# Second attention: the root's function table is loaded directly behind the gate's function

## What is computed

```python
def _L1_attn_ref(x, Wq, Wk, Wv, Wg, Wo, gn_w, gn_b):
    ...
    retention = jnp.einsum('bhsd,bhtd->bhst', q, k) * SCALING
    ...
    out = jnp.einsum('bhst,bhtd->bhsd', retention, v)
    out = out.transpose(0, 2, 1, 3).reshape(B * S, H, Dh)
    mean = out.mean(axis=-1, keepdims=True)
    var = out.var(axis=-1, keepdims=True)
    out = (out - mean) * jax.lax.rsqrt(var + EPS)
    out = out * gn_w.reshape(H, Dh) + gn_b.reshape(H, Dh)
    out = out.reshape(B, S, D)
    gate = jax.nn.silu(x @ Wg.T)
    return gate * out @ Wo.T
```

## Time and profile before

| | |
|---|---|
| three executions | 1035.74, 1040.65, 1041.17 us; median 1040.65 us |
| profiled execution, first to last instruction (span) | 1034.5 us |
| busy in the span: TensorE (matmul), VectorE, ScalarE, GpSimd | 855.4, 859.7, 629.3, 736.5 us |
| the second attention in the span | from 376.5 us (its first table load) to 677.7 us (the next stage's first) |
| one batch of it, once it runs evenly | 17.27 us (from one gate's load at 438.98 us to the next at 456.25 us) |
| function table loads in the whole program | 40, of 1283 ns each, 32 of them in the loop of batches of the second attention |

### The profile page before, as it was taken

The page is one execution under the profiler, slowest core; times in us unless marked ns, Lnnn a source line. Parts: engine busy times, 40 slices in busy tenths (PEclk is TensorE's granted clock), DMA queues, the critical chain, the costliest instruction groups (busy, mean ns, idle before and its releaser), DMA issues. The chain is left out here.

```text
span 1034.5 us, 25463 instructions
## 1 busy us (share of the span) xinstructions
PE 855.4 (83%) x5240; PEld 612.9 (59%) x5240; DVE 859.7 (83%) x2837; ACT 629.3 (61%) x1652; POOL 736.5 (71%) x642
## 2 busy tenths in 40 slices
PE   5699999999969968989898989558888733999993
PEld 4466666666636745555555555335655533999993
DVE  5589999999977976989888889778899861899995
ACT  2655555555429946676767675467765203998992
POOL 4488888888854528999999999655598471355554
PEclk9899999999989979999999999969999755999997
DMA  9520000000000000000000000264567564544420
GB/s 247 172 63 1 0 0 0 0 0 0 1 4 1 1 0 1 11 21 10 20 10 20 10 20 10 59 162 108 167 208 214 185 223 125 151 132 133 134 64 21
DMA packets 64935, 70.11 MB, mean 68 GB/s; under 512 B 8965, under 2 KB 52178, under 8 KB 64740
## 3 DMA queue, kind: packets, MB, share of 16 engines
q1 hardware_dynamic: 50612, 47.20, 16.5%
q0 software_dynamic: 6368, 16.89, 4.8%
q10 hardware_dynamic: 7872, 5.08, 2.0%
HBM read 32.32 MB, written 24.50 MB: 55 GB/s over the span
## 5 line engine op out<-in xcount | busy, mean ns | idle before, releaser
L473 PE MATMUL a_pS<-a_kv,utri 128*128 128x360 f32 (+3 forms) x768 | 263.1, 479 | 17.6 <-POOL a_kv L464 7.2
L464 POOL TENSOR_TENSOR a_kv<-a_qk,a_vv 128x1152 f32<-128x1152 f32 (+1 forms) x128 | 263.9, 2063 | 13.3 <-DVE a_qk L438 13.3
L473 PEld LDWEIGHTS a_pS<-a_kv,utri 128*128 128x128 f32 x768 | 135.5, 190 | 98.8 <-issue 24.6
L569 POOL TENSOR_TENSOR a_tt<-a_tt 128x576 f32<-128x576 f32 (+1 forms) x128 | 156.7, 1225 | 48.2 <-DVE a_tt L553 44.3
L553 DVE TENSOR_TENSOR a_tt<-a_pS,a_qk 128x360 f32<-128x360 f32 (+3 forms) x384 | 180.8, 526 | 9.1 <-PE a_pS L473 6.3
L1950 POOL DMA_INDIRECT out_dram<-x_o,x_place x71 | 69.4, 977 | 75.9 <-DVE x_o L1937 71.4
L581 DVE TENSOR_REDUCE a_nd<-a_tt 128x144 f32<-128x720 f32 (+3 forms) x128 | 104.3, 815 | 0.0
L519 ACT ACTIVATE a_tt<-a_pI 128x144 f32<-128x144 f32 (+1 forms) x96 | 40.1, 417 | 105.3 <-PE a_pI L481 105.2
L512 PEld LDWEIGHTS a_pO<-wgate,a_yT 128*128 128x128 f32 x256 | 44.6, 192 | 75.7 <-issue 42.5
L1530 POOL DMA_INDIRECT ys<-m_S,m_dest x64 | 62.9, 984 | 33.5 <-issue 12.5
L512 PE MATMUL a_pO<-wgate,a_yT 128*128 (+1 forms) x256 | 54.5, 295 | 31.5 <-POOL a_yT L543 22.6
(11 more groups left out here) (299 smaller groups left out, 2187.5 us busy)
## 6 DMA issues: line engine op xcount, KB each, us to landing
x_yl<-ys SPq DMA_DIRECT2D x71, 193.5 KB, 2.5
X<-xs SPq DMA_DIRECT2D x16, 256.0 KB, 5.3
kx<-m_kc SPq DMA_DIRECT2D x64, 64.0 KB
ax<-m_pc SPq DMA_DIRECT2D x64, 64.0 KB
m_S<-X SPq DMA_DIRECT2D x16, 256.0 KB, 4.4
xs<-X SPq DMA_DIRECT2D x15, 256.0 KB
w<-in_L_ffn_W_dram SPq DMA_DIRECT2D x1, 2048.0 KB
m_S<-gw ACTq DMA_DIRECT2D x6, 256.0 KB, 3.2
```

The lines of the kernel that those rows point to most:

```text
L464: pool.tensor_tensor(kv[:, t % 2, :, :, :], kk.unsqueeze(2).to_broadcast([P, H, J, D]), vv[:, t, :, :].unsqueeze(3).to_broadcast([P, H, J, ...
L473: pe.matmul(pS[c][:, 0:(h1 - h0) * SC], K.utri[:, :], flat[:, h0 * SC:h1 * SC], start=True, stop=True).then_inc(u_done, 1)
L569: pool.tensor_tensor(tt[:, t % 2, :, :, D // 2:D], tt[:, t % 2, :, :, D // 2:D], tt[:, t % 2, :, :, 0:D // 2], ALU.add).then_inc(half_done, 1)
```

## The change

One line is added to `act_gate`:

```diff
             act.wait_ge(gate_ps, b + 1)
             wait(act, yT_ready, 4 * (b - 1))
             act.activation(gate[:, half * T:(half + 1) * T], pT[:, :], ACT.Silu).then_inc(gate_ready, 1)
+            act.preload_act_table_set("sqrt_and_others")
```

## The result

The changed kernel took 1052.22 us (median of four runs, 1050.29 to 1053.97) against 1040.91 us before, so by the medians 11.3 us slower. The ratio over all runs is 1.0127, 95% interval 1.0102 to 1.0151. The forecast was 1045.9 us with a range up to 1051 us: the sign was right, the size forecast, 5.3 us, was less than half.

What follows compares the result with a forecast made beforehand. The prediction took the once-per-batch chain root, reciprocal, products, halving as the bound. Its terms, 6.3 - 1.1 + 0.1 = +5.3 us, put on the median 1040.65 us, gave 1045.9 us, range 1038 to 1051 us.

Steps and rivals of the forecast that it cites:

- What bounds the kernel: Second attention, once per batch: the chain root, reciprocal, products, halving holds up even GpSimd, the busiest engine, which idles 0.72 us.
- Gates 1 to 14, +0.45 us each: At these gates `vv` comes 1.42 us later, so VectorE's rotation delays the root by 0.45 us; +6.3 us in all.
- Gate 0, -1.1 us: Start of the second attention: the new load fits ScalarE's 1.35 us pause, and the first root loses its load; -1.1 us.
- Gate 15, +0.1 us: Last gate, with no normalisation between gate and `vv`: the root goes from 650.79 to 650.87 us; +0.1 us.
- The price of the load, 1.30 us, and no second stall: ScalarE behind the gate: the load holds the next function back 1.30 us, with no further drain of 1.38 us.
- the paragraph on TensorE: Transposes wait for `tt`, so `pe_states` moves about 1.42 us; 0 to 0.25 us per gate open, 0 taken.
- TensorE comes late too: Rival: late TensorE work adds 0.25 us more per gate, 3.5 us on top, 1049.4 us; chance 0.15.

## Why the prediction was wrong

**What bounds the kernel:** right. The root, the reciprocal, the products and the halving are the chain; the run with the root ahead of `yaff` shortens the batch by 0.34 us, and VectorE's wait for the root by the same (1.22 to 0.88 us), with only `yaff` moved.

**Gates 1 to 14, +0.45 us each:** right. The clean batches are 0.46 us longer, the wait for `vv` is 1.41 us (1.4 forecast), the one left for the root 0.24 us (0.25), GpSimd's pause 1.11 us (1.17). Two kernels that have this cost and a full clock came out at 1046.37 and 1047.35 us, beside the forecast's 1045.9 us.

**Gate 0, -1.1 us:** right by the profile, -1.2 us (23.88 to 22.68 us from the stage's first load to its first root):

```profile
394.66 1.28 ACT L636 ACT_TABLE_LOAD   x1
...
402.07 0.31 ACT L599 ACTIVATE a_sd<-a_vs,eps 128x16 f32<-128x16 f32 x1
```

The load behind gate 0 lies in ScalarE's pause, and the first root has none of its own. **Gate 15, +0.1 us:** right, 388.4 and 388.5 us from the last gate's load to the end.

**The price of the load, 1.30 us, and no second stall:** right, 1.29 us; the drain that the Trainium skill ("ScalarE: Activation LUTs", section "What ACT_TABLE_LOAD costs") gives beside the load does not show here either.

**The step that failed is the one on TensorE.** The first paragraph read the clock at its full level, and the paragraph on TensorE asked only how late its work would be at that clock: "Between 0 and 0.25 us per gate are therefore open". It took 0 of them, and it did not ask what TensorE's clock does while the engine waits. Before, TensorE had a pause of 0.85 us for GpSimd and none for `tt`; the change moved `tt` by 1.40 us and put a pause of 1.2 to 1.4 us right behind the first. So the term for TensorE, put at nothing, measured 7.8 us: of the 13.0 us between first and last gate, -1.2 us are gate 0's, 14 x 0.46 = 6.4 us the forecast's own, and 7.8 us are what is missing: five batches longer by 1.3 to 1.5 us (7.1 us in all) and 0.6 us at the last. In all six the granted clock is below full. A falling clock was not among the rivals: the one called "TensorE comes late too" had the right engine and the right cause, a late `tt`, but priced it at full clock. In the changed kernel's clean batches that rival is worth nothing; it showed itself only where `tt` came later still.

## What to carry to other kernels

A wait that is moved to another engine is to be priced twice there: by how late it makes that engine's work, and by whether the engine's clock survives the pause; for TensorE, read how much it works around the place before and after, not only whether its results are due. To move a load ahead is free just where the functions that it then holds up have no reader in a hurry: list them with their readers, one by one. And where an in-order list is full, look for something to put behind the critical function before looking for another place for what stands ahead of it.

## What was not expected of the hardware

TensorE's clock fell although the engine was busy 190.51 of 223 us over the stretch and never waited longer than 1.4 us at once in it. Such a pause sufficed in some batches and not in others, and each fall lasted 3 to 4 us.

The second attention's start has the same in it, with no edit of ours. The clock rises to full some 11 us into the stage; in six of the twelve profiles it then fell once more. The windows view of the kernel before, 14 us into the stage (length, TensorE's busy time and count, clock, DMA share, GB/s):

```profile
390.54:392.54 2.00, 1.85 (x7) 1.00 0.00 0
```

and of the kernel with the load behind `vv`, same place:

```profile
391.25:393.25 2.00, 1.84 (x4) 0.62 0.00 0
```

In the executions with that second fall the first root comes 1.6 to 1.7 us later (25.47 to 25.58 us from the stage's first load instead of 23.88; with the load behind gate 0, 24.36 and 24.37 instead of 22.67 and 22.68). It came with and without the change. That it is part of why executions of one kernel here lie microseconds apart is likely but not shown, since only one execution of each kernel was profiled.
